# Gathered probabilities of a sparse attention turned by 64 small identity matmuls per batch in place of 12 SBUF transfers and 3 transposes

## What is computed

```python
I = jnp.where(local[None], jnp.inf, I)
I = jnp.where(causal[None], -jnp.inf, I)
_, idx = jax.lax.top_k(I, kk)
key_c = (c_kv @ W_uk)[bi, idx].reshape(B_, L_, kk, N_HEAD, D_HEAD)
value = (c_kv @ W_uv)[bi, idx].reshape(B_, L_, kk, N_HEAD, D_HEAD)
...
attn = jax.nn.softmax(scores.astype(jnp.float32), axis=-1).astype(v.dtype)
out = jnp.einsum('bhlk,bhlkd->bhld', attn, v)
```

## Time and profile before

| | |
|---|---|
| three runs | 1540.41, 1540.59, 1545.72 us; median 1540.59 |
| the profiled execution | 1545.81 us, span 1544.0 us |
| granted TensorE clock, mean | 0.969 of 2.4 GHz |
| instructions | 30598 |

### The profile page before, as it was taken

How to read it: one execution, slowest core, us unless ns; L and a number is a source line. 1 busy time by engine, 2 the same in 40 slices (tenths; PEclk the granted TensorE clock), 3 DMA queues, 4 the chain that set the end, 5 groups by cost and what they waited for, 6 DMA issues and landing times.

```text
span 1544.0 us, 30598 instructions
## 1 busy us (share of the span) xinstructions
PE 1352.1 (88%) x11816; PEld 966.8 (63%) x11816; DVE 926.0 (60%) x3062; ACT 862.4 (56%) x2231; POOL 324.2 (21%) x420
## 2 busy tenths in 40 slices
PE   5888989898898998988899899888899899888797
PEld 4556657576666566665676566666577567556576
DVE  4755585745565756565366576656446756866634
ACT  3344666554544657545575365754566536665483
POOL 0522030201232211200152112120015310302002
PEclk8989999899999999999999999999999999999999
DMA  8121000000102100000011110000001210000000
GB/s 273 54 61 27 7 1 1 1 4 1 49 21 62 23 5 2 1 1 5 8 42 31 55 23 2 2 1 1 5 8 42 73 24 14 1 1 1 1 1 7
DMA packets 45617, 36.45 MB, mean 24 GB/s; under 512 B 32992, under 2 KB 37536, under 8 KB 44960
## 3 DMA queue, kind: packets, MB, share of 16 engines
q1 hardware_dynamic: 45472, 34.50, 7.8%
HBM read 25.46 MB, written 7.44 MB: 21 GB/s over the span
## 4 chain that ended last, share of the span: by engine, by line
PE 29%; DVE 11%; ACT 7%; issue 2%; POOL 1%; SPq 0%; DMA 0%; POOLq 0%; DVEq 0%; ACTq 0%
PE ps L550 4%; PE ps L757 2%; PE ps L578 2%; ACT arena L1320 2%; PE ps L695 2%; DVE arena L1477 2%; PE ps L743 2%; PE ps L735 2%; DVE small L1726 1%; ACT arena L1114 1%; ACT arena L1268 1%; PE ps L926 1%; PE ps L680 1%; PE ps L1020 1%; PE ps L986 1%
## 5 line engine op out<-in xcount | busy, mean ns | idle before, releaser
L1114 ACT ACTIVATE arena<-ps 128x512 f32<-128x512 f32 (+7 forms) x560 | 251.9, 481 | 229.9 <-PE ps L688 33.2
L550 PE MATMUL ps<-mean_mat 128*128 128x256 bf16 x2038 | 303.4, 282 | 6.8 <-ACT arena L1114 3.4
L550 PEld LDWEIGHTS ps<-mean_mat 128*128 128x128 bf16 x2038 | 192.1, 101 | 97.7 <-issue 55.5
L1901 POOL TENSOR_TENSOR arena<-arena 128x512 f32<-128x512 f32 x64 | 81.3, 1271 | 461.5 <-DVE arena L1497 461.3
L1320 ACT ACTIVATE arena<-arena,small 128x192 f32<-128x192 f32 (+1 forms) x256 | 129.8, 509 | 33.5 <-DVE small L1678 33.0
L1726 DVE TENSOR_REDUCE small<-ps 128x4 f32<-128x1024 f32 x64 | 75.3, 1218 | 25.6 <-PE ps L986 25.3
L1615 DVE TENSOR_TENSOR gath<-ps,rank_tab 96x512 f32<-96x512 f32 x96 | 63.3, 683 | 43.9 <-PE ps L578 43.6
L1779 DVE TENSOR_TENSOR arena<-arena,ps 128x512 f32<-128x512 f32 x64 | 42.8, 686 | 73.1 <-ACT arena L1414 57.9
L1477 DVE CUSTOM_DVE_ANT_0 arena<-ps,mask_w_bf 128x192 f32<-128x192 f32 (+1 forms) x256 | 67.4, 319 | 22.5 <-PE ps L664 22.5
L1370 ACT ACTIVATE arena<-ps 128x512 f32<-128x512 f32 x128 | 66.0, 603 | 23.5 <-PE ps L1020 23.4
L757 PE MATMUL ps<-w_experts,arena 128*128 128x128 f32 x544 | 69.8, 280 | 10.2 <-DVE arena L1779 6.8
(11 more groups left out here) (278 smaller groups left out, 2907.3 us busy)
## 6 DMA issues: line engine op xcount, KB each, us to landing
idxb<-idx_scratch SPq DMA_DIRECT2D x24, 512.0 KB, 5.1
score_scratch<-arena SPq DMA_DIRECT2D x96, 64.0 KB, 1.7
w_experts<-in_experts SPq DMA_DIRECT2D x3, 1088.0 KB, 16.5
w_wqkv<-in_wqkv SPq DMA_DIRECT2D x1, 1536.0 KB, 9.5
arena<-score_scratch SPq DMA_DIRECT2D x96, 16.0 KB, 2.1
arena<-arena SPq DMA_DIRECT2D x96, 16.0 KB, 1.8
arena<-in_x SPq DMA_DIRECT2D x8, 128.0 KB, 2.3
out_x<-arena SPq DMA_DIRECT2D x8, 128.0 KB, 1.9
```

The source lines that it names most:

```text
L550: mm(to, still[:, 0:P], still, start=True, stop=True)
L1114: return act.activation(dst, src, ACT.Copy)
L1901: ins = pool.tensor_tensor(own, own, turned, ALU.add)
```

## The change

The SBUF transfers and `m.xg` go, and the three transposes with them. In slot A5, ahead of `att_values(3)`, PE runs `turn_gathered`: for each head h, tile T and t one f32 matmul whose stationary operand is the block of 32 gathered columns in `probs_a[T]` and whose moving operand is every fourth column of the identity, so that the product is that block turned, for 16 or 32 positions. It goes to bank 1, partitions 32 t to 32 t + 31, columns 48 h on. ACT's four copies into `pdiag` move from slot A6 into slot A5, ahead of the last `u_out` copy, and read bank 1 with the head as the slower index. Six digits of `BUSY`, all of the call that stood in front of the wait for `xg_loaded`, fall to 2: from 5, 6, 7 in rounds 0, 1, 2 of stream 0, from 4, 12, 3 in rounds 0, 2, 3 of stream 1. `TURNS` is as before.

```diff
-        self.xg = three(768, 3, P)
...
-                    if name in ("A2", "A4"):
-                        T = (0, 1)[name == "A4"]
-                        sp.wait_ge(*at("u_prob", 2 * T + 2))
-                        for n in ([0] if T == 0 else [1, 2]):
-                            p0 = LW if n == 0 else LW * (n - 1)
-                            for t in range(GP):
-                                src = m.probs_a[T][p0 + t:p0 + LW:GP, :, keys(T):]
-                                sp.dma_start(m.xg[:, n, RANKS * t:RANKS * t + RANKS], src).then_inc(sig(f"xg_loaded{s}"), 16)
...
+            def turn_gathered():
+
+                pe.wait_ge(*at("u_prob", 4))
+                for h in range(H):
+                    for T in range(2):
+                        rows_, to, n = (slice(LW, P), 0, 16) if T == 0 else (slice(0, P), 16, 32)
+                        for t in range(GP):
+                            last = mm(bank[1][RANKS * t:RANKS * t + RANKS, NG * h + to:NG * h + to + n],
+                                      m.probs_a[T][rows_, h, keys(T):], ident[rows_, rows_.start + t::GP], start=True, stop=True)
+                last.then_inc(*one("xg_turned"))
...
+                    if i == 5:
+                        turn_gathered()
                     if i >= 2:
                         att_values(i - 2)
...
                 keep_busy(bank[2][:, 0:L])
-                pe.wait_ge(*at("xg_loaded", 192))
-                for n in range(3):
-                    last = pe.transpose(bank[2][:, cols(n)], m.xg[:, n, :], ident[:, :])
-                last.then_inc(*one("xg_turned"))
                 pe.wait_ge(*at("u_out", 4))
...
                 for i in range(6):
+                    if i == 5:
+                        act.wait_ge(*at("xg_turned", 1))
+                        act.wait_ge(*at("pdiag_zero", 1))
+                        for t in range(GP):
+                            part = slice(RANKS * t, RANKS * t + RANKS)
+                            ins = copy(m.pdiag[part, :, t, :], bank[1][part, 0:H * NG].rearrange("p (h j) -> p j h", j=NG))
+                        ins.then_inc(*one("pdiag_ready"))
                     if i >= 2:
                         u = i - 2
                         act.wait_ge(*at("u_pv", u + 1))
...
-                act.wait_ge(*at("xg_turned", 1))
-                act.wait_ge(*at("pdiag_zero", 1))
-                for t in range(GP):
-                    part = slice(RANKS * t, RANKS * t + RANKS)
-                    ins = copy(m.pdiag[part, :, t, :], bank[2][part, 0:3 * P].rearrange("p (j h) -> p j h", h=H))
-                ins.then_inc(*one("pdiag_ready"))
                 yield "A6"
```

More of the change, by code:

```diff
@@ L134, in slot_order @@
     return order
-BUSY = [("b0935960007c4ac4135003003811ba0000000201570058454437c00100418390040003500277001305071c906060500620431495211001"
-         "300317082020100663a90081102424044001005000050cca00c07003523230ba11050118a692a72522390001090133c021565001001302"
+BUSY = [("b0935960007c4ac4132003003811ba0000000201570058454437c00100418390040003500277001305071c906020500620431495211001"
+         "300317082020100663a90081102424044001005000050cca00c02003523230ba11050118a692a72522390001090133c021565001001302"
          "0310131ac9820701061260a0b58990000305502c5911200300021570490135704030"),
-        ("06107a50056a6076c2441662759481502011069150b51a724b634403005a194c854057012100247023850218c917021b4403ca5197070b"
-         "40c15479001593005620cc542101535200a0043820093ac2a480c001b60715a25c2310560591a20b6320a422123b68c326014460109070"
-         "5600000c27681430210100608a61610100141301391485c313060031040065008068")]
+        ("06107a50056a6076c2241662759481502011069150b51a724b634403005a194c854057012100247023850218c917021b4403ca5197070b"
+         "40c15479001593005620cc542101535200a0043820093ac2a4802001b60715a25c2310560591a20b6320a422123b68c326014460109070"
+         "5600000c27681420210100608a61610100141301391485c313060031040065008068")]
 GATHERED = ["gscore_mm", "gathT_mm"]
@@ L176 @@
 ALONE = {"x_loaded": 16, "kv_split": 5, "q_ready": 2, "idx_saved": 32, "idx_part0": 16, "idx_part1": 16, "idx_part2": 16, "gsc_saved": 192, "gsc_back0": 64,
-         "gsc_back1": 128, "xg_loaded": 192, "ln_out": 6, "u_mm": 12, "u_bias": 12, "u_exp": 12, "u_prob": 12,
+         "gsc_back1": 128, "ln_out": 6, "u_mm": 12, "u_bias": 12, "u_exp": 12, "u_prob": 12,
          "u_turned": 18, "u_pt_act": 12, "u_pt_dve": 6, "u_pv": 12, "u_out": 12, "x_own": 2, "e_pool": 4, "y_ready": 1,
```

## The result

The changed kernel took 1567.0 us in the median of four runs (1561.4 to 1569.4) beside 1540.5 us for the kernel before in the same session; compared run against run the ratio is **1.0149, with a 95% interval from 1.0126 to 1.0171**: 23 us slower, from 19 to 26. On the 1540.6 us of the prediction that is 1563.6 us. 9 us of the loss were not foreseen. The profiled execution took 1569.0 us with a span of 1567.1, so its sum stands against 1544.0 of before.

The account below looks back on a forecast made before the run. PE's fixed instruction list was taken to bound the kernel. Net PE work +16.6, swallowed waits -1.8 and -0.7, ScalarE +3, given back -3 make +14 us on 1540.6: 1554.6 us, range 1542 to 1564.

Parts of the forecast that it names:

- The bound and the way: Whole kernel: it ends when PE has worked off its fixed list; the change makes it 0.9% slower.
- the read step: Rival for the block: identity columns read 16 bytes apart stream at twice the cost, 0.7 us per batch, 1560 us; chance 0.09.
- Added to PE's list: New block on PE: 128 instructions per batch in 16 runs of 8, 3.0 us per batch, 24.1 us over eight batches.
- the price of the change of form: Inside the block: each switch between the 64x32 and 128x32 tile forms costs 0.107 us.
- Taken from PE's list: At L857: transposes 2.6 us, stalls in front of them 2.2 us, 25 fillers 2.7 us; together 7.5 us less.
- The 2.7 us of filler alone: In front of L857: 25 filler matmuls go, at 0.11 us each.
- Where the block falls into a wait: Behind the block: round 2 stalls swallowed, -1.8 us, and stalls of stream 0's following gather matmuls, -0.7 us; no new wait.
- ScalarE: ACT: the four copies into pdiag, moved ahead of the last u_out copy, delay later work, +3 us together.
- the sign that I gave: In the changed profile, L861 should wait for ACT's copy in rounds 0 and 3 of stream 1.
- Given back later: PE's later waits for the other stream's ACT or DVE chain shrink, an estimated -3 us over eight batches.
- a sign that the forecast was wrong in kind: In the stretches around the block, the granted clock falls from its upper level; no size given.
- SyncE: SyncE's queue: 96 DMA issues go, worth nothing, because the next entry waits for its own data.

Follow-up runs that it names:

- experiment 6: Changed kernel with the new block cut to its last four matmuls (head 7, T = 1), so another output; 1.0004 of the kernel before.
- experiment 3: Changed kernel with the block reading adjacent identity columns instead of every fourth, so another output; 1.0131 of the kernel before.
- experiment 1: Changed kernel with the block's loops exchanged, all heads of T = 0 first, then all of T = 1; 1.0059 of the kernel before.
- experiment 2: Changed kernel with T = 0 also using all 128 rows, so the block has one tile form, order kept; 1.0070 of the kernel before.
- experiment 8: Kernel before, with every second group of four matmuls at L868 using only rows 64 to 127, so another output; 1.0126 of the kernel before.
- experiment 9: experiment 5 with a dense moving operand from a sorted identity copy and the 25 fillers before the last att_values removed; 0.9986 of the kernel before.
- Experiment 10: experiment 6 with ACT's four copies into pdiag back in slot A6, behind the u_out copy; 0.9981 of the kernel before.
- experiment 7: Kernel before with only the six filler digits of the changed kernel (25 fewer fillers), transfers and transposes kept; 1.0013 of the kernel before.
- experiment 4: Changed kernel with the six BUSY digits of the kernel before, so the 25 fillers are back; 1.0170 of the kernel before.
- experiment 5: experiment 2 with ACT's four copies into pdiag and their two waits back at the start of slot A6; 1.0051 of the kernel before.

## Why the prediction was right, and where it was short

- **The bound and the way.** PE's list set the time: 22.9 us more of PE's busy time, 23 us more in all. Without the block the loss is gone (experiment 6).
- **The sum by the page.** The prediction's terms make +18.8 us of work on PE (24.1 - 2.6 - 2.7) and -4.7 us of waits (-2.2 - 1.8 - 0.7 + 3 - 3). Measured are +22.9 us busy and +0.2 us idle. So about 4 of the 9 missing us are work (2.7 the read step, 0.5 changes of form in front of the block, the rest about what the clock can account for) and about 5 are waits. That the forecast still lies within its range is due to the width of the range, not to its terms.
- **Added to PE's list: right in mechanism, too small.** 3.0 us per batch was forecast, 3.35 us was measured (eight blocks of 3.26 to 3.44 us), 26.8 against 24.1 us. With a dense read the eight blocks take 24.0 us (experiment 3): the price of the change of form was right, and the missing 2.7 us are the read step of 16 bytes. It stood among the rivals at 0.7 us per batch and belonged into the sum at half of that; L878, from which I had judged it, did not show it. By run of 8, 0.188 us was forecast, and 0.189 and 0.234 measured. The change itself, put at 0.107 us, is 0.116 in the block and 0.127 at L868. One more change, in front of the block, stood in no term: in the five batches with filler behind the block, that filler comes 3.5 us later behind the work in front of the block than in the kernel before, 0.1 us more than the block's length. With the rule of the Trainium skill ("TensorEngine Tiling (Array Packing)", Key Properties) that a change of tiling mode drains the engine, experiments 1, 2 and 8 agree. The least step of about 25 ns per matmul in the Trainium skill ("TensorE: Matmul & The Clock Gate") does not hold here, where four column groups take turns: 64 matmuls in 128 instructions took 1.14 us in experiment 9.
- **Taken from PE's list: 7.5 us was probably too much.** Experiment 10 measures 2.9 us less than before (0.3 to 5.6), with 8 instructions of the block still in every batch (0.24 us with the change behind them in most, 1.9 us in all): the removal is worth 4.8 us, and by the ends of the interval 2.2 to 7.5. The terms are in the trace (the stalls at L857 are gone), but 1.9 us came back as waits at L940, L682 and L620. I had put at nothing what waits behind `a_out` would do once less work stood in front of them. The 2.7 us of filler alone were worth nothing that can be told (experiment 7).
- **Where the block falls into a wait: right.** The stalls of round 2 (1.8 us) and those of the gather matmuls (0.7 us) are not in the changed profile.
- **ScalarE: right in kind, its sign not seen.** +3 us was forecast; experiments 6 and 10 differ by 3.5 (0.2 to 6.9), with stalls at the two places named. But the sign that I gave, L861 waiting in rounds 0 and 3, is not in the changed profile, nor is the longer wait for the square. There the low clock behind those two blocks slows PE's own work, and the copies come in time. Where the clock stayed full, both waits are there: L861 waits 0.81 and 0.70 us in round 3 of experiments 3 and 4, the square is waited for 0.87, 0.87 and 0.86 us in round 0 of experiments 1 to 3, against 0.47 in the changed kernel and in experiment 4, where the clock is low.
- **Given back later: the step that failed.** I counted -3 us for waits that would shrink. PE's idle time is 191.9 us before and 192.1 after, though 4.7 us of stalls are gone (2.2 at L857, 1.8 and 0.7 under the block). So 4.9 us of waits came up elsewhere, where the prediction's +3 for ScalarE and -3 given back make nothing. 1.4 of them are L940 (0.73 for 0.18) and L682 (0.89 for nothing), as in experiment 10; the others are small and far from the blocks, and not assigned. One reason can be seen: the block lies ahead of the work that PE waits for, so it shifts that work too.
- **What stood in no term: the clock.** The text named a lower clock only as a sign that the forecast was wrong in kind, and the sign appeared: it falls behind 5 of 8 blocks, and each spell stretches what is behind it (nine fillers by 0.8 us). But the sum over the run is small: 4 us more at the lower level in the profiled execution, so at most 2 us of time. And from the changed kernel to one form (experiment 2) the blocks shorten by 13.8 us in all and the time by 12.2. What the spells cost this kernel in its other executions was not measured; in experiment 8 one cost 4 us by itself.
- **SyncE: worth nothing, as forecast**, as far as experiment 10 can tell.

## What to carry to other kernels

Price small matmuls by the forms that stand next to each other and not by their columns: a run that alternates between two tile forms pays 0.12 us at every change, ten times the 9 to 13 ns of one instruction in a run of one form. If a zero in the other operand allows it, widen the narrower form to the wider one; the extra rows were free here. Read the moving operand densely. And before taking away a relay that filler covers, ask what the work that moves up will stand in front of, and which waits behind it the relay and its filler had covered: here four copies of 0.5 us, by the estimate, gave back most of the gain until they went back to their old place, and 1.9 us of the filler and transposes turned into waits.

## What the runs showed that I had not expected

A stretch of PE that is full of changes of form counts as busy in the profile (3.43 of 3.43 us), and yet the granted clock falls to 1.2 GHz behind it: behind 5 of 8 blocks in the changed kernel, 3 of 8 with the filler back and 2 of 8 with the dense read, behind none of 32 with one change or no change inside (experiments 1, 2, 5 and 9), and for up to 13.6 us in experiment 8. Each of these counts is from one execution, and what in such a stretch makes it fall was not measured. And a loss of 22 us hid in a line whose instructions looked alike one by one: the mean duration of an instruction of 32 columns in the block is 229 ns, in experiment 2 233 ns; the distance from start to start tells them apart.
